# Four states a unit turned and summed by TensorE through ScalarE, and the transposes of h left to the DMA queue

## The reference, cut to what matters

```
dA[d,n,l]  = exp(dt[d,l] * A[d,n])
h[d,n,l]   = h[d,n,l-1] * dA[d,n,l] + dt[d,l] * u[d,l] * B[n,l]
y[d,l]     = sum over n of h[d,n,l] * C[n,l]   +  D[d] * u[d,l]
x          = x + tanh(g_x) * y^T * silu(layernorm(x))
hid        = silu(q(x) Wg) * (q(x) Wu)                (2048 wide, q rounds to whole numbers)
x          = x + tanh(g_f) * scale * (q(hid) Wd)
```

## Time and profile before

| | |
|---|---|
| median of 3 runs | 612.37 us |
| the profiled execution | 611.89 us, span 609.9 us |
| busy share of the span | VectorE 91%, GpSimd 85%, TensorE products 85%, ScalarE 83% |
| TensorE's granted clock | full from 190 us on |
| units 5, 6, 7, 9, 10, 13, 14 | 30.3 us each; unit 11: 30.6 us |
| units 8 and 12 | 33.2 us each |

### The profile page before, as it was taken

One profiled execution on the slowest core, in us unless ns is written; L12 is line 12 of the kernel. 1 busy time (PEld: TensorE's weight loads), 2 busy tenths in 40 slices (PEclk: granted clock), 3 DMA queues, 4 the chain that ended last, 5 costly groups with the idle time before them and its releaser, 6 DMA issues. The chain is left out here.

```text
span 609.9 us, 9603 instructions
## 1 busy us (share of the span) xinstructions
PE 516.7 (85%) x3190; PEld 359.8 (59%) x3190; DVE 556.6 (91%) x766; ACT 507.7 (83%) x776; POOL 521.0 (85%) x298
## 2 busy tenths in 40 slices
PE   6999676768675888989879898989789999998997
PEld 2443265747564676767656767675667575764443
DVE  1899989999999899999899999998999999988774
ACT  3879788986999789899978898998798989777773
POOL 1558799999999899999999899999998999973340
PEclk9999859778799999999999999999999999999999
DMA  8992951530661010115521111145411110000323
GB/s 273 403 412 108 325 197 34 192 136 1 240 243 53 0 53 2 35 34 208 203 93 35 34 37 36 35 157 223 121 35 35 36 36 18 1 18 21 84 53 86
DMA packets 38866, 66.32 MB, mean 109 GB/s; under 512 B 12177, under 2 KB 20369, under 8 KB 36002
## 3 DMA queue, kind: packets, MB, share of 16 engines
q1 hardware_dynamic: 38818, 65.72, 30.9%
HBM read 55.49 MB, written 8.13 MB: 104 GB/s over the span
## 5 line engine op out<-in xcount | busy, mean ns | idle before, releaser
L889 POOL TENSOR_TENSOR area_s<-area_s,b_bc 128x1024 f32<-128x1024 f32 x117 | 275.2, 2364 | 14.1 <-DVE u_all L1510 9.9
L515 PE MATMUL pY<-ident,area_s 128*128 128x128 f32 x532 | 87.9, 291 | 54.5 <-DVE area_s L1518 54.5
L584 PE MATMUL pG<-wq_gu,area_f 128*128 128x512 fp8e4 x448 | 108.0, 380 | 4.2 <-ACT area_f L1106 2.9
L1510 DVE TENSOR_TENSOR_SCAN area_s<-pA,area_s 128x512 f32<-128x512 f32 x88 | 105.1, 1205 | 5.1 <-ACT pA L1169 5.1
L515 PEld LDWEIGHTS pY<-ident,area_s 128*128 128x128 f32 x532 | 62.2, 146 | 75.4 <-DVE area_s L1518 67.9
L1169 ACT ACTIVATE pA<-dt_all,a_neg 128x512 f32<-128x512 f32 x145 | 97.7, 682 | 10.7 <-DVE area_s L1510 5.9
L881 POOL TENSOR_TENSOR u_all<-u_all 128x1024 f32<-128x1024 f32 x44 | 103.9, 2361 | 0.2 <-DMA u_all<-bc_rows 0.2
L1518 DVE TENSOR_TENSOR area_s<-area_s,pC 128x512 f32<-128x512 f32 x132 | 87.0, 661 | 0.9 <-DVE area_s L1510 0.8
L509 PE MATMUL pC<-ident,xdT 128*128 128x128 f32 x528 | 84.2, 288 | 3.2 <-DVE area_s L1518 2.0
L584 PEld LDWEIGHTS pG<-wq_gu,area_f 128*128 128x128 bf16 x448 | 41.6, 98 | 48.9 <-ACT area_f L1106 5.2
L509 PEld LDWEIGHTS pC<-ident,xdT 128*128 128x128 f32 x528 | 65.4, 146 | 8.1 <-DVE area_s L1518 6.6
(11 more groups left out here) (218 smaller groups left out, 1123.0 us busy)
## 6 DMA issues: line engine op xcount, KB each, us to landing
b_bc<-bc_rows SPq DMA_DIRECT2D x14, 1024.0 KB, 6.7
area_s<-x SPq DMA_DIRECT2D x32, 256.0 KB, 2.9
u_all<-bc_rows SPq DMA_DIRECT2D x14, 512.0 KB, 6.5
b_bc<-w_gate SPq DMA_DIRECT2D x1, 4096.0 KB, 14.0
dt_all<-x SPq DMA_DIRECT2D x1, 4096.0 KB, 24.3
area_f<-w_up SPq DMA_DIRECT2D x1, 4096.0 KB, 33.6
area_f<-w_down SPq DMA_DIRECT2D x1, 4096.0 KB, 14.9
out<-area_f SPq DMA_DIRECT2D x16, 256.0 KB, 2.1
```

Of the source, the lines that this page charges most:

```text
L515: mm = pe.matmul(pY[:, k * P:(k + 1) * P], src[:, k * P:(k + 1) * P], ident[:, :], is_transpose=True, start=(first and k == 0), stop=(last ...
L584: mm = pe.matmul(bank, xqT[t % 2][:, k, :], wq_gu[:, k, m, c * GW:(c + 1) * GW], start=(k == 0), stop=(k == NT - 1))
L889: gp.tensor_tensor(db[c % NDB], du[s % 2].rearrange("p (a l) -> p a l", a=1).to_broadcast([P, CH, L]), b_bc[:, CH * c:CH * c + CH, :], ALU ...
L1510: dve.tensor_tensor_scan(h, at, dbu, 0.0, ALU.mult, ALU.add).then_inc(S["s_scan"], 1)
```

## The change

From unit 4 on, states 3, 6, 7 and 11 ("turned") leave VectorE's products and GpSimd's `times_c_alone`. TensorE transposes the state itself into a PSUM bank (`h_turn`, four transposes), ScalarE copies it to SBUF (`copy_turned`), and TensorE multiplies it by a diagonal of C and accumulates in pY (`y_turned`, four products of f32). The diagonals are written to DRAM once for each batch element (zeros, then scattered rows of C) and loaded per batch element, 256 KB a state. `diag_d` keeps all four diagonals of D, so `skip` leaves ScalarE from unit 4 on. For all tiles up to 10, `hq_transpose` and `copy_hqT` go; instead ScalarE writes q(hid) in bf16 (`whole_h`, two halves of 1024), and SP issues two transposing transfers a tile (`turn_whole`). Chunks 0 and 2 of the next `gate_silu` wait for these.

```diff
+D_FROM = PLAIN
+TURNED = (3, 6, 7, 11)
-C_STEP = {2: 3, 3: 4, 6: 7, 7: 11, 10: 12, 11: 13, 14: 15, 15: 16}
+C_STEP = {2: 3, 10: 12, 14: 15, 15: 16}
...
+            def scatter_c(b):
+
+                sp.wait_ge(S["c_zero"], 16)
+                for j, n in enumerate(TURNED):
+                    spots = c_diag[b - 1, j].rearrange("(k r) -> k r", k=NT)[:, 0:P * P:P + 1]
+                    sp.dma_start(spots, bc_rows[b, NS + n].rearrange("(k p) -> k p", k=NT), allow_slow_non_contiguous=True).then_inc(S[f"c_cd{b}"], 16)
...
+            def turn_whole(t):
+
+                past(sp, S["f_dn"], t - 1)
+                for i in range(2):
+                    past(sp, S["f_hqD"], 32 * t + 16 * i)
+                    sp.wait_ge(S["f_ha"], 2 * t + i + 1)
+                    sp.dma_start_transpose(hqT[t % 2][:, i * FK // 2:(i + 1) * FK // 2, :], h_int[i]).then_inc(S["f_hqD"], 16)
+
             for s in range(NT, UNITS):
                 load_z(s)
                 load_x(s)
                 load_u(s)
                 if s % NT == 0:
-                    load_b(s // NT)
-                    load_c(s // NT)
-                    load_c_alone(s // NT)
+                    load_b(s // NT, (0, 1, 2))
+                    load_c(s // NT, (0,))
+                if s >= 6:
+                    turn_whole(s - 6)
+                if s % NT == 0:
+                    load_b(s // NT, (3,))
+                    for j in range(ND):
+                        if s > NT:
+                            load_diagonal(s // NT, j)
+                        if j != 1:
+                            load_c(s // NT, ((j or 1),))
```

TensorE's new operations, and its order in a unit (where a unit opens a batch element, gates 0 and 1 stand behind `y_turned(7)`, and `y_sum_pooled(1)` behind gate 3, as it did before):

```diff
+            def h_turn(s, n):
+                pe.wait_ge(S["s_scan"], s * NS + n + 1)
...
+                for k in range(NT):
+                    mm = pe.transpose(h_bank(n)[:, k * P:(k + 1) * P], h_turn_in[at_d(s, n) % 2][:, k * P:(k + 1) * P], ident[:, :])
+                mm.then_inc(S["s_hp"], 1)
+
+            def y_turned(s, n):
+                pe.wait_ge(S["s_hc"], at_d(s, n) + 1)
+                pe.wait_ge(S[f"d_cd{TURNED.index(n)}"], 16 * (s // NT))
+                for k in range(NT):
+                    mm = pe.matmul(pY[:, k * P:(k + 1) * P], diag_c[:, TURNED.index(n), k, :], h_turned[at_d(s, n) % 2][:, k * P:(k + 1) * P],
+                                   start=False, stop=False, skip_group_check=True)
+                mm.then_inc(S["s_yd"], 1)
...
+                h_turn(s, 3)
                 fill(s, early, 4)
-                y_sum(s, 3)
-                c_bcast(s, 6)
                 y_sum_pooled(s, 0)
-                if t2 >= 0:
-                    if t1 % NT:
-                        pe.wait_ge(S["f_xqT"], t1 + 1)
-                    hq_transpose(t2, 0, pG)
-                    hq_transpose(t2, 1, pG)
+                y_turned(s, 3)
                 fill(s, 4, DPARTS)
-                if t2 >= 0:
-                    hq_transpose(t2, 2, pG)
-                    hq_transpose(t2, 3, pG)
-                y_sum(s, 6)
-                c_bcast(s, 7)
+                h_turn(s, 6)
+                h_turn(s, 7)
...
+                    gate(t1, 0)
+                    y_turned(s, 6)
+                    gate(t1, 1)
+                    y_turned(s, 7)
+                    c_bcast(s, 10)
+                    y_sum_pooled(s, 1)
+                    gate(t1, 2)
+                    gate(t1, 3)
                 y_sum(s, 10)
+                h_turn(s, 11)
                 up(t1, 0)
                 up(t1, 1)
                 z_transpose(s)
...
                 y_sum_pooled(s, 2)
+                y_turned(s, 11)
                 c_bcast(s, 14)
                 if s < UNITS - 1:
                     up(t1, 2)
                     du_transpose(s + 1)
                     up(t1, 3)
-                    if s >= PE_FROM:
-                        y_sum_alone(s)
                     y_sum(s, 14)
```

ScalarE, in slot n, and the new wait of `gate_silu`:

```diff
-                    if n == 1:
-                        skip(s)
+                    if n in (5, 8, 9, 12):
+                        copy_turned(s, {5: 3, 8: 6, 9: 7, 12: 11}[n])
...
+                    if n in (6, 7) and t2 >= 0:
+                        whole_h(t2, n - 6)
                     if n in (5, 6) and t2 >= 0:
                         scale_h(t2, n - 5)
...
-                    if n in (7, 8) and t2 >= 0:
-                        copy_hqT(t2, 2 * n - 14, pG)
-                        copy_hqT(t2, 2 * n - 13, pG)
...
-                if t <= UNITS - NT:
-                    past(act, S["f_hqp"], HR * (t - (1 if t < UNITS - NT else 2)) + HR)
-                else:
+                if t < UNITS - NT and t and c % 2 == 0:
+                    act.wait_ge(S["f_hqD"], 32 * (t - 1) + (32 if c else 16))
+                elif t > UNITS - NT:
```

More of the change, by code:

```diff
@@ L56, with turned, at_d @@
 PE_PAIR = 2
-ALONE = 11
-def alone(s, n):
-    return s >= PE_FROM and n == ALONE
+D_FROM = PLAIN
+TURNED = (3, 6, 7, 11)
+ND = len(TURNED)
+def turned(s, n):
+    return s >= D_FROM and n in TURNED
+def at_d(s, n):
+    return ND * (s - D_FROM) + TURNED.index(n)
 def own(s):
-    return [n for n in range(NS) if n // CH not in pooled(s) and not alone(s, n)]
+    return [n for n in range(NS) if n // CH not in pooled(s) and not turned(s, n)]
 OWN_AT = [sum(len(own(i)) for i in range(s)) for s in range(UNITS + 1)]
@@ L222, in build @@
         z_buf = [zn, zt]
+        h_int = [carve(area_f, 1024 * i, F // 4, BF16) for i in range(2)]
         hb = [u_all[:, 2 + 2 * i:4 + 2 * i, :].rearrange("p n l -> p (n l)").bitcast(BF16) for i in range(2)]
@@ L301, in load_u, with load_c @@
                 sp.dma_start(u_in[s % 2], u_rows[s]).then_inc(S[f"d_u{s % 2}"], 16)
-            def load_c(b):
+            def load_c(b, pairs=range(NP)):
                 for j, pair in enumerate(pooled(NT * b)):
+                    if j not in pairs:
+                        continue
                     if b and j < len(pooled(NT * b - 1)):
@@ L523, in y_sum @@
                 pe.wait_ge(S["s_mul"], OWN_AT[s] + m + 1)
-                y_part(p_st[(OWN_AT[s] + m) % NH], first=(m == 0 and s < PLAIN), last=((s < PLAIN or s == UNITS - 1) and n == NS - 1)).then_inc(S["s_ytr"], 1)
+                y_part(p_st[slot(s, OWN_AT[s] + m)], first=(m == 0 and s < PLAIN), last=((s < PLAIN or s == UNITS - 1) and n == NS - 1)).then_inc(S["s_ytr"], 1)
             def y_sum_pooled(s, j):
@@ L609, in late_up @@
                 gate_up(t, c, 1, late_bank(c, 1))
[L611 to L614, removed]
[L615 to L616 removed]
             def down(t, part, z_done):
                 if part == 0:
[L620 to L623 removed]
+                    pe.wait_ge(S["f_hqD"], 32 * t + 16)
                     past(pe, S["f_o"], t)
@@ L692, in _ @@
                 y_skip(s)
-                if s == PLAIN:
-                    c_bcast(s, 3)
-                    y_sum(s, 2)
-                else:
-                    y_sum(s, 2)
-                    c_bcast(s, 3)
+                y_sum(s, 2)
                 if t1 % NT:
@@ L737, in _ @@
                     y_sum_pooled(s, 1)
+                else:
+                    gate(t1, 0)
+                    y_turned(s, 6)
+                    gate(t1, 1)
+                    y_turned(s, 7)
+                    c_bcast(s, 10)
+                    y_sum_pooled(s, 1)
+                    gate(t1, 2)
+                    gate(t1, 3)
                 y_sum(s, 10)
+                h_turn(s, 11)
                 up(t1, 0)
@@ L741, in _ @@
                 z_transpose(s)
-                if ALONE in own(s):
-                    y_sum(s, ALONE)
                 y_sum_pooled(s, 2)
+                y_turned(s, 11)
                 c_bcast(s, 14)
```

152 lines of the change are left out of this document (82 added, 70 removed).

## The result

The changed kernel takes 639.37 us (median of 4 runs, 636.07 to 641.44) against 612.42 us (4 runs, 612.18 to 612.91) before: the ratio is 1.043, with a 95% interval of 1.038 to 1.048. It is slower, as forecast, but by 27 us and not by 13.6. Its profiled execution took 638.05 us, of which the rows cover 635.8.

A forecast was written before the change was run, and what follows sets the result against it. VectorE alone was taken to bound stretch A, VectorE with ScalarE nearly full B, ScalarE C. Growth of 9.6 (ordinary units), 3.4 (units 8 and 12) and 1.2 (unit 15), 14.2 us on 611.89, gave 626 us; range 620 to 631.

The forecast's parts named there:

- ordinary growth of units 5 to 7, 9 to 11, 13, 14: Eight units each grow 0.6 us from ScalarE's work and 0.6 from VectorE's wait for up(3), 9.6 in all.
- units 8 and 12: ScalarE's gap absorbs 1.05 of 1.46 us, adding 0.4; up(3) is 1.3 late: 1.7 us each, 3.4 in all.
- unit 15: Grows by 1.2 us, as unit 9 does.
- unit 4: No h to turn and a fourth times_c lost: taken as 0, bounds -1 to +1 us.
- Bound of the kernel: VectorE and ScalarE wait for each other by stretches; GpSimd, busy 29.91 of 30.34 us, does not bind.
- stretches B and C: B: exponential 7 to 13, 8.56 us, growing 0.6; C: exponential 13 to scan 14, 7.46 us, on ScalarE, cost 0.
- rival 1: GpSimd's queue sets the unit, so unloading it gives 599 us, or 607 in part; chance 0.25 whole or in part.
- stretch A: Scan 14 to the end of the next unit's scan 4, 14.2 us, set by VectorE alone, which has no gap there.
- Stretches B and A: B grows 0.6 us through ScalarE's work; A 0.6 through times_up(3) waiting for up(3) on TensorE.
- The transfers: Transposing transfers are free in ordinary units; behind loads in units 7 and 11 taken as 0, up to 4 us each.
- Rival 4: Transposes queued behind loads in units 7 and 11 delay gate_silu(0) 4 us each, or B's rows are delayed: 634 us; chance 0.10.
- The gap before gate_silu(0) released by a transfer: Sign named in advance that the forecast is wrong and Rival 4 holds; no size given.

The follow-up runs named there:

- e9_clock: e1_queue plus idle TensorE transposes of the identity in units 8 and 12 (8 before turning state 6, 16 before state 7): 632.06 us, ratio 1.033.
- e13_filled: e7_mended with 16 idle transposes ahead of each of h_turn(6) and h_turn(7) in units 8 and 12, down products of parts 3 and 4 moved later: 622.92 us.
- e2_late11: The changed kernel with y_turned(11) moved behind up(3) on TensorE: 635.21 us, ratio 1.037.
- e10_turn15: The changed kernel turning states 2, 11, 15 instead, with e1_queue's SP order and h_turn(15) directly behind up(3): 603.45 us, ratio 0.986.
- e3_short: The changed kernel with copy_turned of states 3, 6 and 7 copying 128 of 512 columns, the rest left out of y: 632.2 us, ratio 1.032.
- e1_queue: The changed kernel with B's rows of states 8 to 11 and C's first pair issued behind the transposing transfers in units 7 and 11: 636.74 us, ratio 1.040.
- e5_turn_queue: e4_turn_only with SP's order of e1_queue: 618.51 us, ratio 1.010.
- e6_turn_busy: e5_turn_queue plus 16 idle transposes of the identity per unit where the 16 transposes of h had been: 612.17 us, ratio 1.000.
- e12_all: e7_mended with e9_clock's idle transposes and, in units 8 and 12, gates 0 and 1 ahead of y_turned(6) and y_turned(7): 626.89 us, ratio 1.022.
- e4_turn_only: The kernel before with whole_h and turn_whole for all tiles replacing hq_transpose and copy_hqT, no turned states: 626.56 us, ratio 1.023.
- e7_mended: The changed kernel with the edits of e1_queue and e2_late11: 628.2 us, ratio 1.026.

## Why the prediction was right and wrong

The growth in the profiled executions is 638.05 - 611.89 = 26.2 us. The prediction's sum had 14.2.

| part | forecast | measured |
|---|---|---|
| ordinary growth of units 5 to 7, 9 to 11, 13, 14 | 9.6 | 8.8 |
| queue, units 7 and 11 (what is over 31.47) | 0 | 6.7 |
| units 8 and 12, growth at the full clock | 3.4 | 4.1 |
| units 8 and 12, clock | 0 | 3.6 |
| unit 15 | 1.2 | 1.3 |
| unit 4, the start, the tail, the rest | 0 | 1.6 |

The ordinary growth is 7 x 1.13 and 0.85 for unit 11, which was 30.62 before. Units 8 and 12 at the full clock are e9_clock's 35.24 less 33.17, twice; the rest of 37.07 and 37.04 is the clock. This split is rough: e13_filled's 34.46 with the 0.56 of e2_late11 put back gives 35.02, so up to 0.4 of the 4.1 may be clock or e9_clock's own added work. The last row: unit 4 0.62, the units before it 0.46, the tail 0.28, and 0.26 outside the span.

- **Bound of the kernel: right.** VectorE's and GpSimd's high busy shares were not the bound. VectorE's saving of 1.74 us in stretches B and C turned into waits, 1.65 us of them counted above. The Trainium skill's advice to optimize the engine of highest occupancy (Perfetto Trace Analysis, Identifying the Most-Contended Engine), rival 1, did not hold: it gave about 600 us. It needs the stretch beside it. e10_turn15 unloads the same engine, in stretch A, and gains 1.07 us a unit.
- **Stretches B and A: right in mechanism and size.** B grew by 0.54, A by about 0.6. e2_late11 took 0.56 away with TensorE's order alone, e3_short 0.87 with ScalarE's work alone.
- **The transfers: the step that failed first.** "The transfers then land some 5 us later, about when the silus want them. I take 0, with up to 4 us a boundary as the other end." By the working's own numbers that is 6.8 + 5 = 11.8 us after exponential 7 against 11.2 wanted, already late, and the term was still put at nothing. The first one landed 13.0 us after exponential 7 (297.1 - 284.07), with three loads of 1 MB ahead of it where the working had 2.5 MB. And the wait stands ahead of the table load, not ahead of the silu, so ScalarE wanted it at 9.8 (292.56 + 1.30 - 284.07). Cost: 5.0 us in unit 7, of which 3.31 are the wait and the rest the slow products behind it (e3_short, at 1.00, paid 3.43 in this unit), and 1.7 in unit 11, all of it the wait. Rival 4 named this mechanism, with its place and near its price; I gave it 0.10. The gap before gate_silu(0) released by a transfer, which the prediction named as its sign, is the row at 297.16. By the Trainium skill (DMA: Bandwidth & Descriptors, Queues, rings and completion order) descriptors are taken in ring order, so transposes wait for the rows issued before them. The trace agrees: 9.1 us to landing behind those loads, at most 4.3 where 1.5 MB of them were moved behind (e1_queue).
- **Units 8 and 12: the step that was missing.** "Of the 1.46 us added, 1.05 goes into it" and up(3) late by 1.3 made 1.7; with the clock held it is 1.85 to 2.07, so that term was 0.2 to 0.4 short. The other 1.8 to 2.0 us a unit come from TensorE's clock, which the working held at the 1.00 of the earlier trace rows. TensorE lost 16 transposes of h per unit; they had stood in the waits of that unit. That the loss of this work takes the clock down is shown without any turned state by e5_turn_queue against e6_turn_busy, where only idle work was put back. With turned states e9_clock, e12_all and e13_filled agree: the longest wait left between the down products and the gates of units 8 and 12 was 1.60, 3.17 and none, and the clock 0.95 or 1.00, 0.91, and 1.00. The longest wait alone does not decide it: the kernel before kept 1.00 with 1.77 us there, and 1.60 went both ways. The Trainium skill (TensorE: Matmul & The Clock Gate, Why this matters for your kernels) warns of idle gaps between bursts of matmuls for this reason. The trace agrees for the long ones, 4.26 us in e4_turn_only and 3.31 us in unit 8 of e10_turn15, and shows the clock down behind shorter waits too. A rival that counts against removing TensorE's work was missing from the prediction.

What stays open: why an ordinary unit (5, 6, 7, 9, 11 or 13) shows 0.95 in some profiled executions and 1.00 in others with the same order of work there. In e1_queue, e2_late11, e7_mended, e9_clock, e12_all and e13_filled the slow products of these units stand at or right behind the wait of 1.98 us for the copy of state 6, which their units at 1.00 have too. That this wait, in whose place unit 9 before had one of 1.07 us, exposes every unit to the drop is likely but not tested, and what tips one unit is not known. The clock does vary between runs of one kernel: e1_queue took 633.21 and 633.8 us at a granted clock of 0.956 in the mean, and 636.6 to 637.25 at 0.938 to 0.944. The four runs of the kernel after spread over 5.4 us, those of the kernel before beside them over 0.7. No run tests what the difference comes from.

## What to carry to other kernels

Look for the stretch that the crowded engine sets alone, and take work from there: the same kind of edit cost 1.13 us a unit in one place (0.57 with TensorE's order mended) and gained 1.07 in another. Before removing work from TensorE, even work off the path, look at which wait it stood in; with that wait left empty, the products behind it ran here at half speed. A transfer on a deadline is issued ahead of bulk loads on its queue, and its deadline is that of the first instruction behind the wait, a table load included.

## What the hardware showed

- TensorE's granted clock fell to 1.2 GHz behind the waits of units 8 and 12 (0.53, 1.87 and 1.14 us in a row in the kernel after, one of 3.17 in e12_all, one of 4.26 in e4_turn_only): behind the last two, eight gate products took 3.60 us in place of 1.90. In unit 8 of e4_turn_only the next eight took 1.89 again.
- With transposes of the identity that nothing reads in those waits, the clock stayed at 1.00 and the kernel was faster, 618.51 to 612.17 us and 603.45 to 600.81.
- A single wait of 1.98 us, followed by the same work, was left at full clock in some units and at half in others.
- A transposing transfer that lands 3.1 us after its issue took 9.1 behind three loads of 1 MB and one of 0.5 MB on the same queue.
